# Cross attention on one core: projections a batch sooner, maxima's by-product in PSUM, rows of maxima sent sooner

## The reference, cut to what matters

```python
qp = x @ Wq.T                         # x: 8 batches x 256 rows x 512
k, v = split(ctx @ Wkv_expand.T)      # ctx: 8 x 256 x 128
scores = einsum("bhqd,bhkd->bhqk", qh, kh) / sqrt(32)    # 16 heads of 32, causal
attn = softmax(scores)
x = layernorm(x + (attn @ vh) @ Wout.T)
```

## Time and profile before

| what | value |
|---|---|
| median of 3 runs | 1060.1 us (1056.87, 1060.1, 1062.93) |
| the profiled execution | 1065.82 us |
| its span | 1064.1 us |
| mean granted clock of PE, as a share of full | 0.977 |
| PE busy | 1005.4 us of the span |
| DVE busy | 669.4 us |
| ACT busy | 454.0 us |
| POOL busy | 261.4 us |

### The profile page before, as it was taken

One profiled execution on the slowest core, in us unless ns is written; L12 is line 12 of the kernel. 1 busy time (PEld: TensorE's weight loads), 2 busy tenths in 40 slices (PEclk: granted clock), 3 DMA queues, 4 the chain that ended last, 5 costly groups with the idle time before them and its releaser, 6 DMA issues. The chain is left out here.

```text
span 1064.1 us, 18069 instructions
## 1 busy us (share of the span) xinstructions
PE 1005.4 (94%) x6352; PEld 857.4 (81%) x6352; DVE 669.4 (63%) x1515; ACT 454.0 (43%) x803; POOL 261.4 (25%) x362
## 2 busy tenths in 40 slices
PE   7899999999979999999979989999999999999996
PEld 5688888888868888887757778989988999778785
DVE  4837546378266677776566837777777775253576
ACT  5523414236125455454534216666665664221210
POOL 4610010103143333333412012312231220503040
PEclk9999999999987999999998989999999999899999
DMA  4503013022786788877622247788778783615042
GB/s 162 194 1 119 0 59 148 0 79 97 210 224 148 218 204 233 232 218 200 212 104 73 82 144 251 246 268 279 236 263 276 253 258 110 221 36 178 19 158 79
DMA packets 87248, 172.79 MB, mean 162 GB/s; under 512 B 8113, under 2 KB 36017, under 8 KB 85393
## 3 DMA queue, kind: packets, MB, share of 16 engines
q1 hardware_dynamic: 81072, 150.21, 45.2%
q0 software_dynamic: 6112, 21.76, 6.2%
HBM read 131.05 MB, written 37.49 MB: 158 GB/s over the span
## 5 line engine op out<-in xcount | busy, mean ns | idle before, releaser
L45 PE MATMUL a_ps_proj<-region_a_rounded,arena 128*128 128x512 f32 x272 | 107.8, 396 | 10.7 <-DVE region_a_rounded L369 6.2
L45 PE MATMUL e_ps_h<-e_x_lo,e_gu_hi 128*128 128x256 f32 (+1 forms) x384 | 110.5, 288 | 3.8 <-DVE e_x_lo L2189 1.3
L962 DVE CUSTOM_DVE_ANT_0 b_dump<-b_ps_s,b_mask 128x128 f32<-128x128 f32 (+1 forms) x256 | 80.3, 353 | 48.5 <-PE b_ps_s L1157 45.3
L46 PE MATMUL e_ps_h<-e_x_hi,e_gu_lo 128*128 128x256 f32 (+1 forms) x384 | 107.5, 280 | 0.0
L47 PE MATMUL e_ps_h<-e_x_hi,e_gu_hi 128*128 128x256 f32 (+1 forms) x384 | 107.4, 280 | 0.0
L46 PE MATMUL a_ps_proj<-region_a_rounded,arena 128*128 128x512 f32 x272 | 106.7, 392 | 0.0
L47 PE MATMUL a_ps_proj<-region_a_rounded,arena 128*128 128x512 f32 x272 | 106.6, 392 | 0.0
L388 DVE SCALAR_TENSOR_TENSOR f_region_b<-a_ps_proj,a_taps,f_region_b 128x510 f32<-128x510 f32 (+2 forms) x96 | 71.7, 746 | 41.0 <-ACT f_region_b L328 38.7
L2195 DVE TENSOR_TENSOR e_gu_lo<-f_region_a,e_gu_hi 128x704 fp32r<-128x704 f32 x92 | 81.2, 886 | 16.6 <-ACT e_gu_hi L2101 16.1
L848 ACT ACTIVATE b_pt<-b_ps_x 128x384 f32<-128x384 f32 x128 | 61.8, 487 | 60.0 <-PE b_ps_x L1181 59.8
L762 POOL TENSOR_SCALAR_AFFINE_SELECT b_pt<-b_pt 128x256 f32<-128x256 f32 x128 | 54.3, 428 | 123.0 <-ACT b_pt L848 122.5
(11 more groups left out here) (418 smaller groups left out, 2665.5 us busy)
## 6 DMA issues: line engine op xcount, KB each, us to landing
f_region_a<-we_gate_up SPq DMA_DIRECT2D x88, 352.0 KB, 5.2
qk_split<-arena SPq DMA_DIRECT2D x24, 512.0 KB, 5.4
y_slots<-f_region_b SPq DMA_DIRECT2D x16, 512.0 KB, 3.7
f_x_next<-x SPq DMA_DIRECT2D x6, 1024.0 KB, 7.4
b_sk<-qk_split SPq DMA_DIRECT2D x24, 256.0 KB, 4.1
b_sq<-qk_split SPq DMA_DIRECT2D x24, 256.0 KB, 5.7
f_region_a<-we_down SPq DMA_DIRECT2D x12, 512.0 KB, 4.4
f_region_b<-we_down SPq DMA_DIRECT2D x11, 512.0 KB, 4.1
```

Source lines behind the costliest of these rows:

```text
L45: pe.matmul(out, a_hi, b_lo, start=first, stop=False)
L46: pe.matmul(out, a_lo, b_hi, start=False, stop=False)
L962: ins = dve.tensor_tensor_reduce(dump[:, n % 2, cols], ps_s[:, n % 2, cols], mask[:, cols], -1.0, 3e38, ALU.add, ALU.min, peak[:, u, k, i: ...
```

## The change

- projected(t) becomes t + 3: the prologue still projects batch 2, rounds 0 to 4 project batches 3 to 7, rounds 5 to 7 project none. The first turn() of round 0 waits for the prologue's last users of ps_pj.
- c_hi and c_lo get a third buffer (CB = GB + 1 = 3); ACT's context() waits for value() of three batches before instead of two, and for nothing while a buffer is fresh.
- maxima() writes its sum back over the scores in PSUM; dump and its wait go.
- peaks(t, 1) stands one head earlier on PE (after head 3 instead of 4), ACT (3 instead of 4) and DVE (4 instead of 5).
- On SP, load_peaks(t + 1, 0) stands ahead of load_stack(t + 2, 0) and of the store of the second half's keys. split_stored becomes a pair, one semaphore for each half.

```diff
@@ -535,6 +535,7 @@
         KH, KL, QH, QL = range(4)
+        CB = GB + 1
 
@@ -547,7 +548,6 @@
         v = sb("v", [P, 2, BT, D])
-        dump = sb("dump", [P, 2, 3 * P])
         peak = sb("peak", [P, 2, BT, UH])
@@ -572,7 +572,7 @@
         xkq_lo_done = sem("xkq_lo_done")
-        split_stored = sem("split_stored")
+        split_stored = pair("split_stored")
         stack_loaded = pair("stack_loaded")
@@ -616,7 +616,7 @@
         def projected(t):
-            return {-1: GB, 0: B}.get(t, t + 2)
+            return t + 3
 
@@ -627,8 +627,8 @@
 
-        def split_count(b, u):
-            return 32 * (2 * (b - GB) + u + 1)
+        def split_count(b):
+            return 32 * (b - GB + 1)
 
@@ -660,17 +660,17 @@
                              split[:, u, KH:KL + 1].rearrange("p s c t -> p s (c t)").bitcast(F32))\
-                    .then_inc(split_stored, 16)
+                    .then_inc(split_stored[u], 16)
 
...
                              split[:, u, QH:QL + 1].rearrange("p s c t -> p s (c t)").bitcast(F32))\
-                    .then_inc(split_stored, 16)
+                    .then_inc(split_stored[u], 16)
 
...
                 if b >= GB:
-                    sp.wait_ge(split_stored, split_count(b, max(u, int(b == GB))))
+                    sp.wait_ge(split_stored[u], split_count(b))
                     sp.wait_ge(e_ready, order(b - 2, u, UH - 1) + 1)
@@ -727,12 +727,12 @@
                     store_q(b, 0)
+                if t >= 0 and real(t + 1):
+                    load_peaks(t + 1, 0)
                 if real(t + 2) and t >= 0:
...
                     store_k(b, 1)
-                if t >= 0 and real(t + 1):
-                    load_peaks(t + 1, 0)
                 if real(b):
@@ -752,7 +752,7 @@
                 pool.wait_ge(c_hi_done, b - GB + 1)
-                pool.tensor_tensor(c_lo[:, b % 2], c_raw[:, (b % 2) * S:(b % 2 + 1) * S], c_hi[:, b % 2].bitcast(F32),
+                pool.tensor_tensor(c_lo[:, b % CB], c_raw[:, (b % 2) * S:(b % 2 + 1) * S], c_hi[:, b % CB].bitcast(F32),
                                    ALU.subtract).then_inc(c_lo_done, 1)
@@ -809,8 +809,9 @@
                     act.wait_ge(inputs_loaded[b % 2], 32 * (b // 2 - 1))
-                act.wait_ge(v_ready, 2 * (b - 2) + 2)
-                act.activation(c_hi[:, b % 2], c_raw[:, (b % 2) * S:(b % 2 + 1) * S], ACT.Copy).then_inc(c_hi_done, 1)
+                if b >= CB:
+                    act.wait_ge(v_ready, 2 * (b - CB) + 2)
+                act.activation(c_hi[:, b % CB], c_raw[:, (b % 2) * S:(b % 2 + 1) * S], ACT.Copy).then_inc(c_hi_done, 1)
 
@@ -822,7 +823,7 @@
                 if b > GB:
-                    act.wait_ge(split_stored, split_count(b - 1, u))
+                    act.wait_ge(split_stored[u], split_count(b - 1))
                 act.activation(split[:, u, KH].rearrange("p c t -> p (c t)"), ps_pj[:, u], ACT.Copy).then_inc(xkq_hi_done, 1)
@@ -908,7 +909,7 @@
                         fill(t, u, i)
-                        if i == 4 and u == 0:
+                        if i == 3 and u == 0:
                             peaks(t, 1)
@@ -955,11 +956,9 @@
                 n = order(b, u, i)
-                if n >= 2:
-                    dve.wait_ge(max_done, n - 1)
                 dve.wait_ge(s_ready, n + 1)
                 for k, cols in ((0, slice(0, P)), (1, slice(P, 3 * P))):
-                    ins = dve.tensor_tensor_reduce(dump[:, n % 2, cols], ps_s[:, n % 2, cols], mask[:, cols],
+                    ins = dve.tensor_tensor_reduce(ps_s[:, n % 2, cols], ps_s[:, n % 2, cols], mask[:, cols],
                                                    -1.0, 3e38, ALU.add, ALU.min, peak[:, u, k, i:i + 1])
@@ -1050,7 +1049,7 @@
                             normalize(t - 1, i - 1)
-                        if u == 0 and i == 5:
+                        if u == 0 and i == 4:
                             peaks(t, 1)
@@ -1078,7 +1077,9 @@
             def turn(b, u):
-                pe.wait_ge(v_done, 2 * (b - 2) + u + 1)
+                pe.wait_ge(v_done, 2 * max(0, b - 3) + u + 1)
+                if b == projected(0):
+                    pe.wait_ge(xkq_lo_done, q_count(GB, 1) if u else k_count(GB, 0))
                 if u == 0 and b >= 2 * GB:
@@ -1096,7 +1097,7 @@
                     mm = three_pass(pe, ps_pj[:, u, c * S:(c + 1) * S], wkv_hi[:, 0, cols], wkv_lo[:, 0, cols],
-                                    c_hi[:, b % 2], c_lo[:, b % 2], True, True)
+                                    c_hi[:, b % CB], c_lo[:, b % CB], True, True)
                 mm.then_inc(xkq_ready, 1)
@@ -1115,7 +1116,7 @@
                 if t == 0:
-                    pe.wait_ge(xkq_lo_done, q_count(GB, 1) if k else k_count(GB, 0))
+                    pe.wait_ge(xkq_lo_done, q_count(p, 1) if k else k_count(p, 0))
                 elif t >= 1 and k == 0:
@@ -1124,7 +1125,7 @@
                 rows = slice(k * P, (k + 1) * P)
-                three_pass(pe, ps_pj[:, k], c_hi[:, b % 2, rows], c_lo[:, b % 2, rows], wkv_hi[:, 1], wkv_lo[:, 1],
+                three_pass(pe, ps_pj[:, k], c_hi[:, b % CB, rows], c_lo[:, b % CB, rows], wkv_hi[:, 1], wkv_lo[:, 1],
                            True, True).then_inc(v_ready, 1)
@@ -1133,8 +1134,8 @@
                         pe.wait_ge(out_added, 2 * b + 1)
-                    elif real(t + 2):
-                        pe.wait_ge(xkq_lo_done, k_count(t + 2, 0))
+                    elif real(projected(t)):
+                        pe.wait_ge(xkq_lo_done, k_count(projected(t), 0))
                     elif t < B:
@@ -1271,7 +1272,7 @@
                             spread_out(t - 1)
-                        if u == 0 and i == 4:
+                        if u == 0 and i == 3:
                             peaks(t, 1)
@@ -2651,10 +2652,10 @@
                 nc.sbuf_tensor("ctx_next", [P, GT], F32) as ctx_next, \
-                nc.sbuf_tensor("c_hi", [P, GB, S], F32R) as c_hi, nc.sbuf_tensor("c_lo", [P, GB, S], F32R) as c_lo:
+                nc.sbuf_tensor("c_hi", [P, GB + 1, S], F32R) as c_hi, nc.sbuf_tensor("c_lo", [P, GB + 1, S], F32R) as c_lo:
             cross = CrossWeights(arena[:], w_q, w_kv, w_o)
             gated_conv(nc, x_t, x_tok, w_in, w_out, conv_w, conv_b, gain, x1, arena[:], cross, sums, conv_ln, ident,
-                       x_next, ctx_t, ctx_next, c_hi, c_lo, split, rounded, own_b)
+                       x_next, ctx_t, ctx_next, c_hi[:, 0:GB], c_lo[:, 0:GB], split, rounded, own_b)
             cross_attention(nc, x1, ctx_t, cross, x2_tiles, conv_ln, ident, x_next, ctx_next, sums, ln,
...
```

## The result

The changed kernel takes 1065.88 us (median of 20 runs, 1059.27 to 1072.4); the kernel before, on the same chips, 1062.01 us (20 runs). The ratio is 1.0037, 95% interval 1.0023 to 1.0051: a little slower, within the 0.5% that counts as no change, but on the other side of zero than the forecast of 1058.8 us, and just above its range. The profiled execution took 1068.0 us (span 1066.3).

The account below looks back on a forecast made before the run. PE's own work was taken to bound full rounds, with room in rounds 0 and 6. Terms -4.1 + 2.3 + 0 + 0.5 + 0 gave -1.3 us, 1058.8 us for the median; range 1052.5 to 1065.5.

Parts of the forecast that it names:

- Order on SP: Stack copies queue behind the rows; hidden except in round 5, where cover is thin: +0.5 us, bounds 0 and +2.
- The rival of the late stack: Stack copies take 8.5 us to land, delaying rounds 0 to 5: +12.1 instead of +0.5, total 1070.4 us; chance 0.08.
- Projections leave round 5: Round 5 loses its set of projections and takes 26.1 for 30.2 us: -4.1 us.
- Projections enter round 0: Round 0 gains a set: first half 11.3 us for 8.1, second 9.8 for 10.7; +2.3 us, bounds -1.3 and +7.4.
- Rows sooner: In rounds 1 to 4, a 0.5 us wait for normalize() replaces a 0.55 us wait for rows: net 0 +-0.1.
- PSUM by-product: DVE's maxima writing PSUM in place: 0 us, bounds -3.4 and +6.7 over 44 instructions where DVE leads.
- The half clock through the first half of round 0: Rival: PE stays at half clock there, round 0 costs +7.4 instead of +2.3: +3.8, 1063.9 us; chance 0.12.
- the two middle rivals: Half clock in round 0's first half (1063.9 us, chance 0.12) and a PSUM surcharge on DVE (1062.1 us, chance 0.12).

Follow-up runs that it names:

- run 1: Changed kernel with SP's order as before, the stack's copies again ahead of the rows of maxima: 1058.45 us, ratio 0.9975 to the kernel before.
- run 2: Changed kernel with SP's order as before and the second half's maxima transposed after head 4 again: 1060.82 us, ratio 0.9985 to the kernel before.
- run 3: Changed kernel with only the second half's maxima transposed after head 4 again, SP's order left as changed: 1068.06 us, ratio 1.0053 to the kernel before.
- Run 8: Changed kernel with SP's order as before in round 5 alone: 1062.42 us, ratio 0.9991 to the kernel before.
- run 4: Kernel before, with only the by-product of the maxima written over the scores in PSUM: 1061.9 us, ratio 0.9992.
- run 5: On top of run 1, the residual of batch 1 loaded late in round 1 instead of at its head: 1058.65 us, ratio 0.9964 to the kernel before.
- run 6: Kernel before, with only the second half's maxima transposed one head sooner on PE, ACT and DVE: 1058.12 us, ratio 0.9951.

## Why the prediction was wrong, step by step

- **Order on SP: the step that failed.** The term was +0.5 us, bounds 0 and +2; by runs 1 to 3 it is 6.6 to 7.4 us. It said that the last copy would land 0.9 us after round 5's end. It landed 2.9 us after PE could have used it, for two reasons: it was issued 22.1 us into the round and not 21.5, and it took 7.5 us to land and not 5.5. The 5.5 us was read from an order in which the other half's copies came 12 us later (420.95 and 433.08); now the residual and the other half stood right behind. The larger mistake was to price such a wait at its own length. The clock stood at half for some 10 us after it, and round 6 took 30.0 us, 3.9 more than before and 5.7 more than in run 1, where the wait is gone. Rounds 0 and 1, where the sum had nothing for the order, took 0.5 to 4 us more than with the order restored; why is open. The rival of the late stack had the mechanism, with chance 0.08. It took 8.5 us to landing, and its price was too high (+12.1), since it charged all of rounds 1 to 4, and in rounds 2 to 5 PE never waited for the stack.
- **Without that term** the forecast would be -1.8 us, a ratio of 0.9983. That lies in the interval of run 1, the changed kernel with SP's order restored, and of run 2. It does not show each of the other terms right: two errors below offset each other in part.
- **Round 1** was not in the sum. In the first profile a store, six copies of the stack and two residuals stood ahead of the rows of round 1: 2.4 us of wait, 5.2 us of round. By the five profiles in the section on the result this belongs to the projections' stores in round 0 rather than to SP's order, and so to the term of the projections; no run isolates it. Run 8, the same kernel up to there, shows that this varies (0.8 us, and a longer round 0).
- **Projections leave round 5**, -4.1: measured -3.6 (26.6 us), and -4.2 from run 4 to run 2. Right. With full clock throughout such a round takes 24.3 us (runs 1 and 5), so the 26.1 us read from round 6 of before held a fall of the clock.
- **Projections enter round 0**, +2.3: measured +4.3 here (24.2 to 28.5 us), +3.0 in run 1. The first half came out at 11.9 us for 11.3, the second at 11.2 for 9.8, with the clock at 0.85. From run 4 to run 2 it is +4.2 in round 0 and +0.7 in round 1. The direction was right, the size too small by about half. The times of these two runs are 1061.9 and 1060.8, 0.1% apart. That this work gains little where engines are already busy was the core of the forecast, and holds.
- **Rows sooner**: both waits were right to 0.1 us (0.5 us for normalize(), 0.55 gone). The net of 0 was too low a gain: alone the edit is worth 5 us (0.9951, clear of noise), beside the others 2.2 to 2.4 (not clear of noise). Why it is worth more than the waits is open.
- **PSUM by-product**: taken as 0 within -3.4 and +6.7; measured 0.9992. Each instruction with 256 columns takes 44 ns more and the accumulator's read 58 ns more, yet from one head's first instruction to its end DVE needs only 0.04 us more. The Trainium skill, page "Perfetto Trace Analysis", section "Optimizing Scalar/DVE Operations", gives about 60 ns of overhead on SBUF and 125 on PSUM, 65 ns more; the trace agrees in direction, with less in steps from one instruction to the next, and the time does not show it.
- The half clock through the first half of round 0 did not come: 1.00 there, 0.85 in the second half.
- The range reached up to 1065.5, which covers each of the two middle rivals but not both together: 1058.8 + 5.1 + 3.3 is 1067.2. The measured 1065.9 just above it came by neither of them.

## What to carry to other kernels

A time to landing holds for the copies that are in flight beside it. When an issue is moved, look up which groups of copies will then be back to back, and ask what the last of them and the smallest behind them (here 8 KB that PE waits for) will take. Issue large copies as soon as their buffers are free and never behind a wait on an engine that has nothing to do with them; and price a wait on PE with the fall of its clock after it, which here about doubled it: 2.4 us of wait and 5.2 us of round in round 1, 2.9 and 5.7 in round 6 (against run 1). Take a round that depends on when copies bunch up from more than one profile: round 1 took 35.3, 34.5 and 30.6 us with the same instructions.

## What was not expected

A small copy can pay for large ones issued before it: from the end of the issue of the rows, two copies of 8 KB, to PE's next instruction it took 1.4 us in a quiet round (412.14 + 1.43 to 414.96) and 5.7 in round 1 of the changed kernel (350.77 + 1.44 to 357.93). With the second residual moved away (run 5) PE does not wait in round 1 at all.

A light round varies by execution: without a large wait it takes 24.3 to 24.7 us in the profiles of runs 1, 2, 4, 5, 6 and 8, and 25.5 to 27.0 in others, or in another round of the same execution. One round of one execution is no sure price.

DVE's accumulator read takes 140 ns after an output to PSUM, 82 ns after one to SBUF.
